# Two-layer-norm matmul on eight cores: coefficient rows copied after the second W block, second pair's results placed elsewhere

## The chip, the cores and the metric

The kernel runs on all 8 cores of one Trainium2 chip. Each core works alone on 1024 of 8192 token rows; nothing is exchanged between cores. The metric is the device time of the slowest core in microseconds (us), as the median of repeated runs. Engine names: TensorE (PE in the profile) multiplies, VectorE (DVE), ScalarE (ACT) and GpSimd (POOL) do the rest, SyncE (SP) only issues transfers. Each engine takes its own instructions strictly in program order, DMA issues and semaphore waits included.

## What is computed

```python
x = L0_attn_x                                  # [1, 8192, 4096], float32
x = x + attn(layernorm(x))                     # one batch entry: softmax over a single element is 1,
                                               # so this is x + layernorm(x) + layernorm(x)
x = x + layernorm(x) @ (aa * tanh(kk * W)).T + bias      # W is [4096, 4096]
```

With one batch entry the attention weighs a single element, so the first step is a per-token scale and shift of x, and the second layer norm is again one. Both are folded into coefficients per token (`cf`, `s1a`, `b1a`). What remains is one matmul of the normalized x with tanh(kk W), plus a residual that is linear in x, plus the bias.

## The kernel before, in words

**Two ways of multiplying.** The first 1024 output columns (`DS`) are made plainly, in two blocks `ot` = 0 and 1 of 512 columns, for 8 token tiles `t`: a closed group (t, ot) is 16 pieces `p` of two matmuls of 512 columns each. The other 3072 columns are made in 12 pairs `j` of 256 columns by a seven-product scheme (`PRODUCTS` M5, M3, M4, M2, M6, M7, M1, 16 matmuls each, 112 a pair), transposed: the product's rows are output columns. This scheme needs sums of quarters of the normalized x (`sA5`, `sA2`, `sA1` and two in place, made once by VectorE, `add_tile`) and sums of blocks of tanh(W) for every pair (`sums`: S6, D12, S1, S7, D21, made by VectorE). Each product is added by VectorE (`take`) into the pair's four result quarters `C(j, q)`, which start as the residual: x transposed, loaded by GpSimd (`load_xt`), times the coefficient row `srow`, plus the row `brow` (`residual`, two GpSimd operations for a quarter). `srow` and `brow` come from TensorE, which spreads the per-token coefficients over all partitions (order entries `("R", 0)` and `("R", 1)`), and from ScalarE, which copies them out of PSUM (`copy_rows(0)`, `copy_rows(1)`).

**Order of TensorE.** `tensor_order` writes it out: token tiles are transposed (`"T"`) as they arrive; block 0 of each follows; in between and after, block 1 of tiles 0 to 4 (`EARLY` = 5) goes piece by piece (`second(p)`), then block 1 of tiles 5 to 7, then the 12 pairs.

**W.** 128 loads of 512 KB (pieces `w`) go through a ring of 4 buffers (`wr`). Pieces 0 to 31 are blocks 0 and 1, then 8 for each pair. SyncE issues the load of piece w when ScalarE has done the tanh of piece w-4. ScalarE does `TANH_BEFORE[t]` pieces before it normalizes its half of tile t, evicts the transposed tile, and goes on; the first rows are copied just ahead of piece 27 and the second just ahead of piece 30. A wait for TensorE's rows therefore holds the tanh, and with it the ring.

**GpSimd's queue.** In program order: half of the normalization, the 8 stores `serve(0..7)` of block 0, the reloads of x for block 1, `load_xt(0, q)` for four quarters, `residual(0, q)`, the 8 stores `serve(8..15)` of block 1 (each waits for VectorE's eviction), `load_xt(1, q)`, `residual(1, q)`, and then for every pair the loads and residuals one and two pairs ahead, where a load waits until ScalarE's store of the pair two before has landed.

**Memory.** Two regions, `early` and `late`, are used again by stage. `base[t]`, the plain results of tile t, stand at `late` 32 + 2t (in units of 512 bf16 columns, two units each). Pair 1's (and every odd pair's) quarters stood at `late` 40 to 47 and its S6 and S7 at 32 and 36. So `load_xt(1, q)` waits for all 8 tiles' results to have landed in memory, and VectorE's S6 of pair 1 waits for those of tiles 0 to 3.

Of the kernel before, what the change touches and what calls it, by code (L numbers as in the profile page):

```python
# [9 lines left out]
F32 = mybir.dt.float32  # L10
# [9 lines left out]
NT = TOK // 128  # L20
# [22 lines left out]

TANH_BEFORE = [1, 4, 7, 10, 13, 16, 20, 23]

# [14 lines left out]
EARLY = 5  # L60

def tensor_order():

    todo = []
# [37 lines left out]
    for p in range(7, PPB):  # L104
        todo += second(p)
        if p in (9, 12):
            todo.append(("R", (9, 12).index(p)))
    for ot in range(1, NO):
# [5 lines left out]
def build_nc():  # L114
# [37 lines left out]

    CT = [[part(early, 32 + 4 * o, 4, F32) for o in range(2)], [part(late, 40 + 4 * o, 4, F32) for o in range(2)]]

# [4 lines left out]
    slot = {}  # L159
    for i, n in enumerate(["B22", "B12", "B11", "B21", "S6", "S7"]):  # L160
        slot[n, 0], slot[n, 1] = part(early, 48 + 4 * i, 4), part(late, 16 + 4 * i, 4)

# [157 lines left out]
    def _(gpsimd):  # L320
# [27 lines left out]
        def load_xt(j, q):  # L348

            if j == 0:  # L350
                gpsimd.wait_ge(s_tr, NCH * NT)
            elif j == 1:
                for t in range(NT):
                    gpsimd.wait_ge(s_y[t], 16 * NO)
            else:
                gpsimd.wait_ge(s_so[j % 2, q], 16 * (j // 2))
            r = 256 * j + 128 * q[1]
            gpsimd.dma_start(C(j, q), xt_h[r:r + 128, 512 * q[0]:512 * (q[0] + 1)]).then_inc(s_xt[j % 2, q], 16)
# [12 lines left out]
        for q in QUARTERS:  # L371
            residual(0, q)
        for i in range(NT, NG):
            serve(i)
        for q in QUARTERS:
            load_xt(1, q)
        for q in QUARTERS:
            residual(1, q)
# [15 lines left out]
    def _(vector):  # L394
# [95 lines left out]
        def sums(j, names):  # L490

            p = j % 2
            for n in names:
# [4 lines left out]
                if n == "S6" and j == 1:  # L498

                    for t in range(4):  # L500
                        vector.wait_ge(s_y[t], 16 * NO)
# [91 lines left out]
    def _(scalar):  # L593
# [43 lines left out]
        while w < W0:  # L637
            if w in (27, 30):
                copy_rows((27, 30).index(w))
            tanh_piece(w)  # L640
            w += 1
        def store(j, q, read):
            scalar.wait_ge(s_rd, READS * j + read)
# [3 lines left out]
        for j in range(NP + 1):  # L647
# [6 lines left out]
            for b in BLOCKS:  # L654
                if j < NP:
                    for k in range(2):
                        scalar.wait_ge(s_w[w % RING], 16 * (w // RING + 1))
                        scalar.activation(slot[b, j % 2][:, k * PW:(k + 1) * PW], wr[w % RING][:, :],  # L658
                                          AF.Tanh, bias=0.0, scale=kk[:, :]).then_inc(s_wt, 1)
                        w += 1  # L660
                if b == "B22" and j >= 2:
                    store(j - 2, (0, 0), 11)
                    store(j - 2, (1, 1), 12)
# [119 lines left out]
```

## Time and profile before

| | |
|---|---|
| runs, median (lowest to highest) | 474.29 us (473.62 to 475.14), 3 runs |
| profiled execution | 478.1 us |
| its span (slowest core, core 3) | 476.6 us |
| spans of the 8 cores | 464.5 to 476.6 us |
| TensorE busy in the span | 433.9 us, 91% |
| VectorE, ScalarE, GpSimd busy | 319.1, 194.2, 203.6 us |

The span is from the first to the last instruction of a core. The profiled execution's own time is 1.5 us above its slowest span and 3.8 us above the median of the runs. A row of a timeline merges neighbours of one kind: start, duration, engine, line, operation, output and inputs by name, how many, and in brackets the idle time ahead of it and what ended that.

### The profile page before, as it was taken

What the parts mean: (1) busy time and instruction counts of PE and PEld (TensorE: products, weight loads), DVE (VectorE), ACT (ScalarE), POOL (GpSimd) and SP (SyncE); (2) the same over time, 40 slices, a digit from 0 to 9 for tenths busy, and PEclk for the clock granted to TensorE, in tenths of its full rate; (3) what the DMA queues carried; (4) which work ended last, traced back from release to release, by engine and by line L of the source; (5) the groups of instructions that cost most, each with busy time, mean ns of one, the idle gap of its engine ahead of it and who ended that gap; (6) DMA issues with size and microseconds to landing.
All of it is one profiled execution on the core that took longest, in us unless ns stands there. A gap on an engine that the chain in (4) does not pass through costs nothing.

```text
span 476.6 us, 7052 instructions; the slowest of 8 cores (464.5 to 476.6 us)
## 1 busy us (share of the span) xinstructions
PE 433.9 (91%) x2184; PEld 205.3 (43%) x2184; DVE 319.1 (67%) x474; ACT 194.2 (41%) x181; POOL 203.6 (43%) x188
## 2 busy tenths in 40 slices
PE   0555899999997999999998999899999999999996
PEld 0533445554543444444443444344444444444442
DVE  2688777687536399998158842978296858584852
ACT  0387777745634604252511541343335242424000
POOL 0132212124153611284366454765566655675620
PEclk9969899999999999999999999999999999999999
DMA  6999999975899878968866976698969796967221
GB/s 134 315 314 302 301 339 290 288 237 157 240 268 289 263 222 242 281 172 343 223 197 227 278 289 221 192 301 287 282 202 305 266 295 218 329 189 270 77 78 45
DMA packets 36612, 116.37 MB, mean 244 GB/s; under 512 B 5088, under 2 KB 5088, under 8 KB 36576
## 3 DMA queue, kind: packets, MB, share of 16 engines
q1 hardware_dynamic: 23472, 84.43, 57.2%
q0 software_dynamic: 5760, 18.88, 13.9%
q10 hardware_dynamic: 7344, 12.62, 7.1%
q8 instruction: 18, 0.29, 0.3%
q14 instruction: 18, 0.15, 0.1%
HBM read 99.14 MB, written 16.78 MB: 243 GB/s over the span
## 4 chain that ended last, share of the span: by engine, by line
PE 48%; DMA 22%; issue 7%; DVE 6%; POOLq 5%; DVEq 5%; POOL 4%; ACT 3%; SPq 1%; ACTq 0%
PE acc L735 34%; PE acc L715 12%; DMA early<-x 6%; DMA wr<-wpieces 6%; DMA early<-xt 5%; POOLq L365 5%; PE acc L686 2%; DMA y<-late 2%; DVEq L464 2%; DMA late<-xt 2%; POOL early L366 2%; POOL late L366 2%; DVEq L517 1%; DVE stats L413 1%; DVE early L509 1%
## 5 line engine op out<-in xcount | busy, mean ns | idle before, releaser
L658 ACT ACTIVATE late<-wr,kk_sb 128x1024 bf16<-128x1024 f32 x48 | 52.9, 1142 | 109.1 <-DVE early L519 39.7
L735 PE MATMUL acc<-h2T,late 128*128 128x512 bf16 x384 | 85.2, 379 | 2.6 <-DVE late L509 2.6
L735 PE MATMUL acc<-h2T,early 128*128 128x512 bf16 x384 | 84.8, 379 | 0.0
L658 ACT ACTIVATE early<-wr,kk_sb 128x1024 bf16<-128x1024 f32 x48 | 53.4, 1143 | 73.3 <-DVE early L522 20.4
L522 DVE SCALAR_TENSOR_TENSOR early<-acc,early 128x512 f32<-128x512 f32 x48 | 33.2, 692 | 56.9 <-POOL early L366 31.0
L715 PE MATMUL acc<-early,h2T 128*128 128x512 bf16 x256 | 60.4, 387 | 4.2 <-ACT early L599 4.2
L715 PE MATMUL acc<-late,h2T 128*128 128x512 bf16 x256 | 58.9, 387 | 3.3 <-ACT late L599 3.3
L735 PEld LDWEIGHTS acc<-h2T,late 128*128 128x128 bf16 x384 | 37.4, 98 | 48.6 <-issue 4.0
L735 PEld LDWEIGHTS acc<-h2T,early 128*128 128x128 bf16 x384 | 37.6, 98 | 45.3
L366 POOL TENSOR_TENSOR early<-early 128x512 f32<-128x512 f32 x24 | 36.0, 1499 | 44.3 <-DMA early<-xt 21.9
L509 DVE TENSOR_TENSOR early<-early 128x2048 bf16<-128x2048 bf16 x30 | 44.8, 1495 | 9.5 <-ACT early L658 7.6
L326 POOL TENSOR_SCALAR early<-early,cf 128x1024 bf16<-128x1024 f32 x12 | 17.4, 1453 | 74.8 <-DVE cf L440 74.8
L509 DVE TENSOR_TENSOR late<-late 128x2048 bf16<-128x2048 bf16 x30 | 47.7, 1590 | 1.7
L522 DVE SCALAR_TENSOR_TENSOR late<-acc,late 128x512 f32<-128x512 f32 x48 | 33.2, 692 | 22.8 <-PE acc L735 12.9
L364 POOL TENSOR_TENSOR early<-early 128x512 f32<-128x512 f32 x24 | 32.9, 1373 | 34.8 <-DMA early<-xt 34.8
L364 POOL TENSOR_TENSOR late<-late,early 128x512 f32<-128x512 f32 x24 | 38.4, 1600 | 17.5 <-DMA late<-xt 17.4
L735 PE MATMUL acc<-early 128*128 128x512 bf16 x192 | 43.4, 379 | 0.0
L735 PE MATMUL acc<-early,late 128*128 128x512 bf16 x192 | 43.4, 379 | 0.0
L366 POOL TENSOR_TENSOR late<-late,early 128x512 f32<-128x512 f32 x24 | 35.2, 1468 | 17.8 <-DMA late<-xt 8.6
L715 PEld LDWEIGHTS acc<-late,h2T 128*128 128x128 bf16 x256 | 25.1, 99 | 33.6 <-issue 6.5
L413 DVE BATCH_NORM_STATS2 stats<-early 128x6 f32<-128x512 f32 x48 | 29.6, 680 | 13.4 <-DMA early<-x 12.7
L715 PEld LDWEIGHTS acc<-early,h2T 128*128 128x128 bf16 x256 | 24.5, 99 | 32.4 <-issue 7.0
(58 smaller groups left out, 425.7 us busy)
## 6 DMA issues: line engine op xcount, KB each, us to landing
wr<-wpieces SPq DMA_DIRECT2D x128, 512.0 KB, 8.0
early<-x SPq DMA_DIRECT2D x24, 512.0 KB, 15.4
early<-xt POOLq DMA_DIRECT2D x24, 256.0 KB, 7.1
yt<-early ACTq DMA_DIRECT2D x24, 256.0 KB, 3.7
late<-xt POOLq DMA_DIRECT2D x24, 256.0 KB, 4.6
yt<-late ACTq DMA_DIRECT2D x24, 256.0 KB, 5.9
h2T<-x SPq DMA_DIRECT2D x8, 512.0 KB, 17.8
y<-late POOLq DMA_DIRECT2D x16, 256.0 KB, 5.2
```

The source lines that it names most:

```text
L326: gpsimd.tensor_scalar(h2b[:, c * CW:(c + 1) * CW], x_of[t][:, c * CW:(c + 1) * CW], cf[t % 2][:, 0:1], cf[t % 2][:, 1:2], ALU.mult, ALU.a ...
L364: gpsimd.tensor_tensor(c, c, srow[:, cols], ALU.mult)
L365: gpsimd.drain()
L366: gpsimd.tensor_tensor(c, c, brow[:, cols], ALU.add).then_inc(s_bs[q], 1)
L413: vector.bn_stats(stats[:, 6 * k:6 * k + 6], x_of[t][:, 512 * k:512 * (k + 1)])
L464: vector.drain()
L509: vector.tensor_tensor(slot[out, p], slot[a, p], slot[b, p], op).then_inc(s_wc, 1)
L522: vector.scalar_tensor_tensor(c, bank, float(sign), c, ALU.mult, ALU.add).then_inc(s_rd, 1)
L658: scalar.activation(slot[b, j % 2][:, k * PW:(k + 1) * PW], wr[w % RING][:, :], AF.Tanh, bias=0.0, scale=kk[:, :]).then_inc(s_wt, 1)
L686: mm = tensor.transpose(ptr[i % 2][:, q * 128:(q + 1) * 128], h2b[:, c * CW + q * 128:c * CW + (q + 1) * 128], ident[:, :])
L715: mm = tensor.matmul(acc[bank_of[t, ot]][:, :], h2T[:, t * D + k * 128:t * D + (k + 1) * 128], wp[ot % 2][:, k * 512:(k + 1) * 512], start ...
L735: mm = tensor.matmul(acc[pbank[j, m]][:, :], slot[b, j % 2][:, k * 128:(k + 1) * 128], a[:, :, k * 128:(k + 1) * 128], start=(k == 0), sto ...
```

## The change

Six edits. (1) ScalarE does three more tanh pieces (23, 24, 25) ahead of its half of tile 7. (2) It copies no rows between pieces any more: the first rows are copied after piece 31, the second after the four tanh pieces of B22 and B12 of pair 0. (3) TensorE's second spreading stands one piece row later, after `second(13)` instead of `second(12)`. (4) The odd pairs' quarters move to `late` 32 to 39, over the results of tiles 0 to 3; S6 and S7 of odd pairs move to 40 and 48. (5) `load_xt(1, q)` waits for tiles 0 to 3 only and is issued after store 12, ahead of the stores 13 to 15. (6) VectorE's S6 of pair 1 waits for tiles 4 and 5 instead of 0 to 3.

```diff
-TANH_BEFORE = [1, 4, 7, 10, 13, 16, 20, 23]
+TANH_BEFORE = [1, 4, 7, 10, 13, 16, 20, 26]
...
-        if p in (9, 12):
-            todo.append(("R", (9, 12).index(p)))
+        if p in (9, 13):
+            todo.append(("R", (9, 13).index(p)))
...
-    CT = [..., [part(late, 40 + 4 * o, 4, F32) for o in range(2)]]
+    CT = [..., [part(late, 32 + 4 * o, 4, F32) for o in range(2)]]
...
-        slot[n, 0], slot[n, 1] = part(early, 48 + 4 * i, 4), part(late, 16 + 4 * i, 4)
+        slot[n, 0], slot[n, 1] = part(early, 48 + 4 * i, 4), part(late, (16, 20, 24, 28, 40, 48)[i], 4)
...
             elif j == 1:
-                for t in range(NT):
+                for t in range(4):
                     gpsimd.wait_ge(s_y[t], 16 * NO)
...
-        for i in range(NT, NG):
+        for i in range(NT, NT + EARLY):
             serve(i)
         for q in QUARTERS:
             load_xt(1, q)
+        for i in range(NT + EARLY, NG):
+            serve(i)
         for q in QUARTERS:
             residual(1, q)
...
                 if n == "S6" and j == 1:
-                    for t in range(4):
+                    for t in range(4, 6):
                         vector.wait_ge(s_y[t], 16 * NO)
...
         while w < W0:
-            if w in (27, 30):
-                copy_rows((27, 30).index(w))
             tanh_piece(w)
             w += 1
+        copy_rows(0)
...
                         w += 1
+                if b == "B12" and j == 0:
+                    copy_rows(1)
```

What the edits do to ScalarE's row of work around tile 7, before. L599 is a tanh piece of the two plain blocks, L607 the normalization, L617 the eviction of the transposed tile, L635 a copy of coefficient rows, L658 a tanh piece of the pairs:

```order
L599 ACTIVATE late<-wr,kk_sb 128x1024 x3
L607 ACTIVATE early<-early,cf 128x1024 x2
L617 COPY h2T<-acc 128x1024 x4
L599 ACTIVATE late<-wr,kk_sb 128x1024 x4
L635 COPY early<-acc 128x512 x2
L599 ACTIVATE late<-wr,kk_sb 128x1024 x3
L635 COPY early<-acc 128x512 x2
L599 ACTIVATE late<-wr,kk_sb 128x1024 x2
L658 ACTIVATE early<-wr,kk_sb 128x1024 x8
```

And of the change, the same place (lines 601, 609, 619, 637 and 659 are the same statements):

```order
L601 ACTIVATE late<-wr,kk_sb 128x1024 x6
L609 ACTIVATE early<-early,cf 128x1024 x2
L619 COPY h2T<-acc 128x1024 x4
L601 ACTIVATE late<-wr,kk_sb 128x1024 x6
L637 COPY early<-acc 128x512 x2
L659 ACTIVATE early<-wr,kk_sb 128x1024 x4
L637 COPY early<-acc 128x512 x2
L659 ACTIVATE early<-wr,kk_sb 128x1024 x4
```

Three tanh pieces moved ahead of the normalization of tile 7, and both pairs of copies moved behind all tanh of block 1.

GpSimd's queue between the residual of pair 0 and that of pair 1, before. L334 is a store of plain results, L358 a load of x transposed, L364 and L366 the two operations of a residual quarter; s_y are the landed stores of a tile:

```order
L366 TENSOR_TENSOR early<-early 128x512
L334 DMA y<-late 128x512 [waits s_ev] x8
L358 DMA late<-xt 128x512 [waits s_y0,s_y1,s_y2,s_y3,s_y4,s_y5,s_y6,s_y7] x4
L364 TENSOR_TENSOR late<-late,early 128x512 [waits s_xt101]
L366 TENSOR_TENSOR late<-late,early 128x512
```

And of the change:

```order
L366 TENSOR_TENSOR early<-early 128x512
L334 DMA y<-late 128x512 [waits s_ev] x5
L358 DMA late<-xt 128x512 [waits s_y0,s_y1,s_y2,s_y3] x4
L334 DMA y<-late 128x512 [waits s_ev] x3
L364 TENSOR_TENSOR late<-late,early 128x512 [waits s_xt101]
L366 TENSOR_TENSOR late<-late,early 128x512
```

The four loads now stand ahead of the last three stores and wait for four tiles instead of eight; the residual operations still stand behind all stores.

TensorE around the two spreadings (L700, later L703), before; L715 (L718) are the plain matmuls:

```order
L715 MATMUL acc<-late,h2T 128x512 x30
L700 MATMUL acc<-early,ones 128x512 x6
L715 MATMUL acc<-late,h2T 128x512 x30
L700 MATMUL acc<-early,ones 128x512 x6
L715 MATMUL acc<-late,h2T 128x512 x126
```

And of the change:

```order
L718 MATMUL acc<-late,h2T 128x512 x30
L703 MATMUL acc<-early,ones 128x512 x6
L718 MATMUL acc<-late,h2T 128x512 x40
L703 MATMUL acc<-early,ones 128x512 x6
L718 MATMUL acc<-late,h2T 128x512 x116
```

The second spreading moved ten matmuls down.

## Rows read from the trace of the kernel before

**Rows 1.** The head of the page.

```profile
span 476.6 us, 7052 instructions; the slowest of 8 cores (464.5 to 476.6 us)
```

**Rows 2.** Span and mean granted TensorE clock of core 6.

```profile
core 6: 472.9 us, clock 0.974
```

**Rows 3.** Timeline of TensorE, core 3: start, duration, what, idle ahead.

```profile
118.62 1.06 PE L686 MATMUL acc<-ident_sb,early 128*128 128x128 bf16 x16
...
152.88 24.73 PE L715 MATMUL acc<-late,h2T 128*128 128x512 bf16 x106 [3.29 <-ACT late L599]
177.45 3.62 PE L735 MATMUL acc<-early 128*128 128x512 bf16 x16
...
205.07 7.07 PE L735 MATMUL acc<-h2T,late 128*128 128x512 bf16 x32
```

**Rows 4.** What TensorE waited for after 130 us, core 3: total us, times, longest.

```profile
PE acc L715 <- ACT late L599: 3.3, 1, 3.3
PE acc L735 <- DVE late L509: 2.6, 3, 1.3
PE acc L735 <- DVE early L509: 1.3, 2, 0.9
```

**Rows 5.** The same view of core 6, its only wait.

```profile
PE acc L715 <- ACT late L599: 2.4, 1, 2.4
```

**Rows 6.** Timeline of ScalarE, core 3.

```profile
108.13 3.23 ACT L599 ACTIVATE late<-wr,kk_sb 128x1024 bf16<-128x1024 f32 x3
114.10 2.37 ACT L607 ACTIVATE early<-early,cf 128x1024 bf16<-128x1024 f32 x2 [2.75 <-DVE cf L440]
...
136.95 1.23 ACT L635 COPY early<-acc 128x512 f32<-128x512 f32 x2 [9.28 <-PE acc L700]
138.08 3.23 ACT L599 ACTIVATE late<-wr,kk_sb 128x1024 bf16<-128x1024 f32 x3
...
151.59 1.15 ACT L599 ACTIVATE late<-wr,kk_sb 128x1024 bf16<-128x1024 f32 x1 [4.59 <-DMA wr<-wpieces]
```

**Rows 7.** Load of W piece 25, core 3: issue time, and time to landing.

```profile
L291 SPq DMA_DIRECT2D wr<-wpieces x1: 328/328/328, 110.4 to 110.4; - x1
...
DMA to landing us min/median/max: 7.3/7.3/7.3
```

**Rows 8.** The same load on core 6.

```profile
L291 SPq DMA_DIRECT2D wr<-wpieces x1: 327/327/327, 112.4 to 112.4; - x1
...
DMA to landing us min/median/max: 4.6/4.6/4.6
```

**Rows 9.** Timeline of TensorE, core 6: transposes of tile 7.

```profile
120.61 1.06 PE L686 MATMUL acc<-ident_sb,early 128*128 128x128 bf16 x16
```

**Rows 10.** Timeline of GpSimd, core 3.

```profile
196.90 0.55 POOL L358 DMA_DIRECT2D late<-xt  x1 [9.70 <-DMA y<-late]
...
201.37 1.27 POOL L364 TENSOR_TENSOR late<-late,early 128x512 f32<-128x512 f32 x1 [1.11 <-DMA late<-xt]
...
214.40 1.26 POOL L366 TENSOR_TENSOR late<-late,early 128x512 f32<-128x512 f32 x1
...
241.74 1.26 POOL L366 TENSOR_TENSOR early<-early 128x512 f32<-128x512 f32 x1 [1.92 <-issue]
```

**Rows 11.** Timeline of VectorE, core 3.

```profile
163.55 2.54 DVE L509 TENSOR_TENSOR early<-early 128x2048 bf16<-128x2048 bf16 x2 [7.61 <-ACT early L658]
...
203.29 3.58 DVE L509 TENSOR_TENSOR late<-late 128x2048 bf16<-128x2048 bf16 x2
...
243.22 1.48 DVE L522 SCALAR_TENSOR_TENSOR early<-acc,early 128x512 f32<-128x512 f32 x2 [15.14 <-PE acc L735]
```

**Rows 12.** Line 509 (the block sums), 180 to 320 us: ns min/median/max.

```profile
L509 DVE TENSOR_TENSOR late<-late x15: 1215/1225/2267, 198.4 to 315.3; 128x2048 bf16<-128x2048 bf16 x15
```

**Rows 13.** Transfers by line, from the page: KB each, median us to landing.

```profile
wr<-wpieces SPq DMA_DIRECT2D x128, 512.0 KB, 8.0
early<-x SPq DMA_DIRECT2D x24, 512.0 KB, 15.4
```

More of the change, by code:

```diff
@@ L151, in build_nc @@
     sA5, sA2, sA1 = part(early, 0, 16), part(early, 16, 16), part(late, 0, 16)
-    CT = [[part(early, 32 + 4 * o, 4, F32) for o in range(2)], [part(late, 40 + 4 * o, 4, F32) for o in range(2)]]
+    CT = [[part(early, 32 + 4 * o, 4, F32) for o in range(2)], [part(late, 32 + 4 * o, 4, F32) for o in range(2)]]
     def C(j, q):
```

## The prediction, as made before the change was run

> **What bounds the kernel now.** I read the page first: the span is 476.6 us, that of core 3 [rows 1]. Then the waits of TensorE on core 3: after 130 us it stands still for three reasons only, 3.3 us for a tanh of ScalarE and 2.6 and 1.3 us for block sums of VectorE (line 509) [rows 4]. That makes 7.2 us; all the rest of that stretch is matmul after matmul, so TensorE is the bound, and a microsecond there counts only if it is one of these 7.2 or a new one. Core 6, with a span of 472.9 us [rows 2], has but one of the waits, 2.4 us for the same tanh [rows 5]. So cores differ, and the time is that of the slowest.
>
> The timelines tell where the two kinds come from. The tanh wait stands at 152.88 us, ahead of the last piece row of block 1 [rows 3]. ScalarE had no data: its last tanh of the block began at 151.59 us after 4.59 us of waiting for the W load [rows 6]. That load goes out when piece 27 is done, and piece 27 began at 138.08 us, because ScalarE had stood 9.28 us for TensorE's coefficient rows before it [rows 6]. The wait for the rows emptied the W ring.
>
> The waits for VectorE start at GpSimd. Its loads for pair 1 went out at 196.90 us, after 9.70 us in which it waited for the last plain stores to land; so the last of those was issued by 187.2 us. Its residual of pair 1 ran from 201.37 to 215.7 us [rows 10]. From there it is late for all that follows: the second residual quarter of pair 2 was finished by the operation at 241.74 us [rows 10], and VectorE, idle for 15.14 us, took pair 2's first product at 243.22 us [rows 11]. The row puts this idle time down to TensorE, but the product had ended near 229 (TensorE starts a product every (205.07 - 177.45) / 8 = 3.45 us, so product M5 of pair 2 runs from 225.8 to 229.2 [rows 3]). What came last was GpSimd. With 14 us lost, VectorE handed over its sums too late five times.
>
> **The change, part by part.** (a) No rows between the tanh pieces. Pieces 26 to 31 follow the eviction of tile 7. Piece 27 is then done some 11 us sooner than now, and so is the load of piece 31, where 3.3 us were missing: all of that wait goes, on core 6 too. The copies themselves (1.23 us for two [rows 6]) are the same work elsewhere. The second spreading waits for the first copies, which come right after the first spreading at 137 us plus, or when piece 31 is done. Piece 31 is asked for when 27 is done, near 128 us; even at the 15.4 us of an x load [rows 13] the copies would be through by 128 + 15.4 + 1.15 + 1.23 = 146 us. TensorE comes to the last piece row at 152.88 - 3.29 = 149.6 us now [rows 3], and the second spreading stands ten matmuls (24.73 / 106 x 10 = 2.3 us) and its own six ahead of it, so at 147.8 us with the 1.8 us of (b). Cost: nothing; with that cover gone, what the copies are late.
>
> (b) Three more tanh pieces ahead of tile 7's normalization. That is the price. Piece 25 is loaded at 110.4 us on core 3 and lands 7.3 us later, at 117.7 [rows 7]; its issue hangs on the tanh of piece 21 (in the group at 108.13 [rows 6]) and doesn't move. Its tanh takes 1.15 us and half of a normalization 2.37 / 2 = 1.2 us [rows 6], so the first quarter of tile 7 is ready at 120.05 us instead of 115.3. TensorE wants it at 118.62 [rows 3]: 1.5 us of new wait with the hand-over. ScalarE then has the second half of the normalization to do before it evicts the first transposes; I add 0.3 us and get 1.8. On core 6 the load of piece 25 goes out at 112.4 us and lands 4.6 us later [rows 8]; 117.0 + 1.15 + 1.2 = 119.4, ahead of the 120.61 us at which its TensorE arrives [rows 9]: nothing there. Bounds of this cost: nothing, and, with the landing of the x loads of the same size, 15.4 us instead of 7.3 [rows 13], 9.9 us. I take the rows' own 1.8 since the load is issued as before; piece 27's load, issued 1.1 us after piece 26's instead of after tile 7, comes behind it.
>
> (c) The second spreading 2.3 us later, and 1.8 us from (b), hold VectorE's second sum of quarters, on which its next work follows. But VectorE then stood 7.61 us before its first block sums at 163.55 us, waiting for a tanh [rows 11], that (a) brings 10 us forward. It starts them at 163.55 - 7.61 + 4.1 = 160.0, 3.5 us sooner. TensorE reaches the pairs 3.3 - 1.8 = 1.5 us sooner, so VectorE gains 2 us on it.
>
> (d) Pair 1's loads ahead of the last three stores. They wait for the stores of tiles 0 to 3 only. With up to 9.7 us for a store to land [rows 10], I put their issue near 176 us and their landing before the last store. The residual of pair 1 then follows that store, near 182 us instead of 201.37: 19 us sooner, done by 182 + 14.3 = 196. Behind them in GpSimd's queue stand the three stores; these wait for evictions later than that anyway. From here every load of pair 2 waits for ScalarE's store of pair 0 instead of GpSimd's backlog. M5 of pair 2 could be taken up to 14 us late before a wait arose; 14.0 us late is what it is now, and I expect under 3. The 3.9 us of waits for line 509 go.
>
> (e) VectorE's sum S6 of pair 1 now waits for the store of tile 5, issued third from last, near 176; it lands by 186. VectorE comes to it behind pair 0's takes, at 198.4 now [rows 12] and 3.5 us sooner then: hidden by 8 us. The new places themselves cost nothing: sizes are as before.
>
> (f) GpSimd's residual of pair 1 now runs beside VectorE's sums from 182 to 196 us. A sum in line 509 takes 1.215 us at least, and up to 2.267 [rows 12]. The two sums at 203.29 us, beside that residual, took 3.58 instead of 2.43 [rows 11]. I give it 2 us in all. These two end at 206.9 now, 206.9 - 3.5 + 2 = 205.4 after, and TensorE wants them for M4 of pair 1, at 205.07 + 3.45 = 208.5 now and 207.0 after [rows 3]. 1.6 us are left. Bounds: nothing, or each of the eight residual operations of 1.27 us [rows 10] held against VectorE in full, 10.2 us.
>
> The Trainium skill, SBUF — State Buffer, section "SBUF: two separate sides", speaks against this part: the port pair that VectorE and GpSimd share is an exclusive lock for a whole instruction, for VectorE operations with two SBUF inputs too. The longest sum of line 509, 1.05 us over the shortest [rows 12], is about what a lock held through a residual operation would do; by that rule in its worst case the sum has the 10.2 us of (f), as the fourth rival below has it.
>
> **The sum.** Core 3: 476.6 - 3.3 - 3.9 + 1.8 = 471.2. Core 6: 472.9 - 2.4 = 470.5. The slowest falls by 5.4 us. The profiled execution is 478.1 us, 3.8 above the median of the runs shown, so its slowest core has perhaps more of these waits than the slowest of a usual run. If that were like core 6, it would gain 2.4. I take 4.3, between the two and nearer to the worked sum: 474.3 - 4.3 = **470.0 us**.
>
> **The rivals.** First, the forecast with a slowest core like core 6: 2.4 us, 471.9 us. For it: the 3.8 us between the profile and the runs. Second, only the tanh wait goes: VectorE, shared with GpSimd, is as late for the sums as now, since TensorE came sooner too. Core 3 then gains 3.3 - 1.8 = 1.5, time 472.8 us. For it speaks the thin 1.6 us of (f). Against it: the five waits now follow a lateness of 14 us. Third, slower: piece 25 lands late, as it shares the transfers with one more load. The place is the transposes of tile 7. At 15.4 us to landing [rows 13], core 3 pays 9.9 us for the 7.2 it gains: 476.6 + 2.7, which is 477.0 us in a run. It decides from 12.7 us to landing on; below that it only shortens the gain. Against it: 7.3 and 4.6 us are what this load took [rows 7, 8], in a stretch with few transfers. Fourth, the 10.2 us of (f): the two sums would end at 213.6, and M4 of pair 1 wait 6.6 us; core 3 stands at 477.8, a run at 475.5 us. Fifth, the change doesn't do what it says: the stores of tiles 0 to 3 land so late that the loads hold the last three stores and the residual starts no sooner. Then it gives the time of the second.
>
> **How the numbers follow.** Forecast 0.58; first rival 0.15; second and fifth together 0.14; third 0.06; fourth 0.07. A measurement of this kernel tells from no change about 0.3%, 1.4 us. Faster by more than that: forecast and first rival, and half of the second, 0.80. Within it: the other half, and some of the fourth, 0.12. Slower: third and the rest of the fourth, 0.08. The forecast's own range is 467.5 to 471.5. Range: from 466.3, all 7.2 us and no new wait with a little beside, up to 473.4, past the second rival.
>
> **What would show it.** In the profile after: no wait for ScalarE in line 718 after 130 us; one of 1 to 2 us at tile 7's transposes on core 3, none on core 6; the tanh pieces of block 1 all done by 136 us; pair 1's residual from about 182 us; VectorE's idle time ahead of pair 2's first take under 8 us, and no wait of TensorE for line 509 after 220 us. Wrong would be: a tile 7 wait over 3 us on several cores, waits for block sums in pairs 0 and 1, or spans that fall on core 3 while another core, from its first 70 us, holds the time.

## The result, and the profile after

The changed kernel takes 478.1 us, the kernel before 474.29 us, medians of 9 runs each: a ratio of 1.0081, interval 1.0045 to 1.0117. It is slower by 0.8%; 470.0 us was forecast, with a chance of 0.80 of a gain.
The profiled execution of the changed kernel took 478.21 us, close to its median; that of before was 3.8 us above its own. So the equal spans of the two profiles don't mean equal times:

```profile
span 476.6 us, 7034 instructions; the slowest of 8 cores (463.5 to 476.6 us)
```

What TensorE waited for after 108 us on the slowest core, now core 2 (total us, times, longest):

```profile
PE acc L738 <- DVE late L511: 5.0, 4, 2.2
PE acc L738 <- DVEq L582: 2.3, 1, 2.3
PE acc L738 <- DVEq L568: 1.4, 1, 1.4
PE acc L689 <- ACT early L609: 0.7, 1, 0.7
PE acc L738 <- DVE early L511: 0.2, 1, 0.2
```

Against [rows 4] the wait for a tanh (there line 599, here it would be line 601) is gone. In its place stand 8.9 us of waits for VectorE instead of 3.9. L511 is the line of the block sums (509 before); L582 is where VectorE reports sA1, the sum of tiles that the last product of pair 0 reads; L568 is its report of the tile differences ahead of it. Together 9.6 us, where core 3 of before had 7.2.

Where they fall, from TensorE's timeline on core 2:

```profile
116.77 1.05 PE L689 MATMUL acc<-ident_sb,early 128*128 128x128 bf16 x16 [0.74 <-ACT early L609]
...
185.87 7.07 PE L738 MATMUL acc<-h2T,early 128*128 128x512 bf16 x32 [1.37 <-DVEq L568]
195.26 5.29 PE L738 MATMUL acc<-late,early 128*128 128x512 bf16 x16 [2.33 <-DVEq L582]
...
210.69 3.61 PE L738 MATMUL acc<-h2T,late 128*128 128x512 bf16 x16 [2.24 <-DVE late L511]
```

Tile 7 costs 0.74 us, below the 1.8 us of the forecast. The rest begins where the pairs begin, and falls in pairs 0 and 1. That is VectorE's and GpSimd's stretch, so I read their timelines next. VectorE, core 2:

```profile
161.89 7.84 DVE L490 TENSOR_TENSOR h2T<-h2T 128x2048 bf16<-128x2048 bf16 x4
169.91 4.24 DVE L511 TENSOR_TENSOR early<-early 128x2048 bf16<-128x2048 bf16 x2 [0.19 <-issue]
...
185.90 1.48 DVE L524 SCALAR_TENSOR_TENSOR early<-acc,early 128x512 f32<-128x512 f32 x2 [0.45 <-issue]
...
202.04 2.54 DVE L511 TENSOR_TENSOR late<-late 128x2048 bf16<-128x2048 bf16 x2 [5.39 <-DMA y<-late]
```

The first row is the first four of the eight in-place differences of the transposed input, the second two block sums behind them (S7 and D21). The same two groups before, on core 3 (lines 488 and 509):

```profile
170.68 4.62 DVE L488 TENSOR_TENSOR h2T<-h2T 128x2048 bf16<-128x2048 bf16 x4
175.49 2.54 DVE L509 TENSOR_TENSOR early<-early 128x2048 bf16<-128x2048 bf16 x2 [0.19 <-issue]
```

The four differences took 4.62 us then and 7.84 us now, the two sums 2.54 and 4.24. VectorE had begun the pairs' work well ahead: its first block sums (S6 and D12) start at 153.77 us on core 2, against 163.55 [rows 11]. From there to the first take, at 185.90 against 187.68 us, it has no idle time worth naming in either kernel, and 8.0 of the 9.8 us are lost: 3.2 and 1.7 in the two groups above, 1.1 in the fifth difference and 1.0 in each of two plain results. GpSimd, core 2, tells why:

```profile
155.92 1.50 POOL L364 TENSOR_TENSOR early<-early 128x512 f32<-128x512 f32 x1 [15.48 <-DMA early<-xt]
162.79 1.44 POOL L366 TENSOR_TENSOR early<-early 128x512 f32<-128x512 f32 x1 [5.37 <-issue]
...
175.42 2.07 POOL L366 TENSOR_TENSOR early<-early 128x512 f32<-128x512 f32 x1
177.44 2.72 POOL L334 DMA_DIRECT2D y<-late  x5
189.49 0.55 POOL L358 DMA_DIRECT2D late<-xt  x1 [9.33 <-DMA y<-late]
...
192.12 1.61 POOL L334 DMA_DIRECT2D y<-late  x3
194.97 1.26 POOL L364 TENSOR_TENSOR late<-late,early 128x512 f32<-128x512 f32 x1 [1.24 <-DMA late<-xt]
204.46 1.27 POOL L366 TENSOR_TENSOR late<-late,early 128x512 f32<-128x512 f32 x1 [8.23 <-issue]
```

Pair 0's residual (lines 364 and 366, eight operations) runs from 155.92 to 177.5 us, on top of VectorE's differences and sums from 161.89 on. Before, on core 3, it ran from 147.31 to 161.4, its last four operations in the 7.61 us in which VectorE stood idle for a tanh [rows 11]; the block sums and differences from 163.55 on ran without it. The stores 8 to 12 (block 1 of tiles 0 to 4) go out in one heap at 177.44, since they stand behind this residual. Those of before, on core 3:

```profile
147.31 1.55 POOL L364 TENSOR_TENSOR early<-early 128x512 f32<-128x512 f32 x1 [7.66 <-DMA early<-xt]
152.00 1.27 POOL L366 TENSOR_TENSOR early<-early 128x512 f32<-128x512 f32 x1 [3.13 <-issue]
...
161.38 1.12 POOL L334 DMA_DIRECT2D y<-late  x2
```

The first two left at 161.38 us then, the others as VectorE had their results. So pair 1's loads now leave at 189.49 us and the store of tile 5, which VectorE's S6 of pair 1 now waits for, behind them; VectorE stands 5.39 us for it at 202.04.

Why did the residual of pair 0 start so late? Its four loads were issued at about the same time, 138.3 to 139.9 us against 137.5 to 139.1; counted from tile 7's transposes that is 2.6 us later, and the larger part is the landing. Their landing after (core 2), and then before (core 3):

```profile
DMA to landing us min/median/max: 17.5/18.9/21.9
```

```profile
DMA to landing us min/median/max: 9.7/10.7/11.9
```

I read it so that the W loads, which ScalarE now lets go earlier, share the transfers with them. One experiment below (x4) bears on it; it was not measured apart, and stays argued.

To compare kernels without the differences of single cores, I took from each profile the mean over its 8 cores, counted from the start of tile 7's transposes (T). "Pairs" is TensorE's first product, "sums" VectorE's first block sums, "take" its first take, R0 and R1 the residuals of pairs 0 and 1, "waits" the sum of TensorE's waits after 108 us. The kernels e1 to x4 are those of the experiments below.

```
kernel   pairs  sums   take   R0 start, length   R1 start   waits
before   56.2   42.2   66.8   27.9, 14.8         78.1       3.5
after    53.8   37.3   67.2   35.8, 19.5         73.2       4.1
e1       53.7   37.4   66.6   34.9, 19.3         78.1       3.9
e2       54.9   41.8   66.4   27.8, 14.8         66.0       2.8
e3       53.7   37.6   66.6   34.2, 18.8         68.9       3.4
e4       53.8   38.1   66.8   29.8, 23.8         70.1       3.9
e5b      53.8   37.4   65.1   34.4, 14.9         65.1       4.7
e6b      55.3   42.0   66.4   27.9, 14.1         76.7       2.0
e7b      53.8   37.0   61.1   35.6,  9.1         61.4       0.9
e8b      55.4   43.1   67.2   27.8,  6.4         76.6       2.5
e9       53.7   41.5   70.1   37.2, 18.6         73.9       6.1
x1       53.7   37.5   75.8   34.5, 15.3         65.9       3.8
x2       56.0   42.3   72.7   28.0, 14.0         75.8       2.1
x4       53.7   41.1   72.1   29.1, 13.3         74.4       1.7
```

TensorE reaches the pairs 2.4 us sooner after the change, and VectorE starts its block sums 4.9 us sooner; its first take is no sooner. That difference is the case. (In x1, x2 and x4 the first take was moved behind other work, so theirs is another thing.)

A wait of TensorE can cost more than its length. On core 2 the 16 matmuls behind the wait of 2.33 us took 5.29 us, others 3.61. The granted clock, the last figure but two of this row of busy times, was 0.57 of full speed there, so mostly the lower of the two levels, and 1.00 in the 4 us before and after:

```profile
195.00:199.00 4.00, 3.74 (x10) 1.40 (x11) 1.39 (x2) 0.00 (x0) 1.22 (x1) 0.57 1.06 242
```

Five of the eight cores have one such group in the pairs, 1.4 to 1.7 us longer. Before, on core 3, the same stood behind the 3.29 us for the tanh [rows 3]: 0.58 from 153 to 157 us. In e7b, where no core waits over 1.1 us in the pairs, seven cores end 348.0 to 348.2 us after T; after the change they end 349.3 to 359.8 us after it.

### The profile page after: what moved, and what is told of

The parts are those of the page before. It is cut to its first block, busy times and chain, and to the rows that moved or that the text cites. A ratio compares the mean times of both kernels' runs of the same rounds, so it can differ in the third digit from the quotient of the medians.

```text
span 476.6 us, 7034 instructions; the slowest of 8 cores (463.5 to 476.6 us)
## 1 busy us (share of the span) xinstructions
PE 435.8 (91%) x2184; PEld 205.6 (43%) x2184; DVE 328.0 (69%) x474; ACT 193.7 (41%) x181; POOL 207.7 (44%) x188
## 3 DMA queue, kind: packets, MB, share of 16 engines
q0 software_dynamic: 5760, 18.88, 14.9%
## 4 chain that ended last, share of the span: by engine, by line
PE 44%; DMA 25%; issue 10%; POOLq 7%; POOL 6%; DVE 3%; DVEq 2%; SPq 2%; ACT 1%; ACTq 0%
PE acc L738 34%; DMA early<-xt 8%; PE acc L718 8%; DMA wr<-wpieces 8%; POOLq L365 6%; DMA y<-late 4%; DMA early<-x 3%; POOL early L366 3%; DMA late<-xt 2%; POOL late L366 2%; PE acc L689 2%; SPq L285 2%; DVEq L519 1%; DVEq L507 1%; ACT early L609 1%
## 5 line engine op out<-in xcount | busy, mean ns | idle before, releaser
L718 PE MATMUL acc<-early,h2T 128*128 128x512 bf16 x256 | 61.7, 393 | 2.9 <-ACT early L601 2.9
L738 PEld LDWEIGHTS acc<-h2T,late 128*128 128x128 bf16 x384 | 37.3, 98 | 51.3 <-issue 7.1
L718 PE MATMUL acc<-late,h2T 128*128 128x512 bf16 x256 | 57.0, 379 | 0.0
L366 POOL TENSOR_TENSOR early<-early 128x512 f32<-128x512 f32 x24 | 36.5, 1522 | 46.3 <-DMA early<-xt 22.6
L364 POOL TENSOR_TENSOR early<-early 128x512 f32<-128x512 f32 x24 | 37.1, 1548 | 41.5 <-DMA early<-xt 41.4
L511 DVE TENSOR_TENSOR late<-late 128x2048 bf16<-128x2048 bf16 x30 | 48.0, 1600 | 7.0 <-DMA y<-late 5.4
L511 DVE TENSOR_TENSOR early<-early 128x2048 bf16<-128x2048 bf16 x30 | 48.4, 1615 | 1.8 <-issue 0.2
L524 DVE SCALAR_TENSOR_TENSOR late<-acc,late 128x512 f32<-128x512 f32 x48 | 33.2, 692 | 21.9 <-POOL late L366 11.5
L366 POOL TENSOR_TENSOR late<-late,early 128x512 f32<-128x512 f32 x24 | 35.5, 1479 | 24.5 <-issue 12.2
L364 POOL TENSOR_TENSOR late<-late,early 128x512 f32<-128x512 f32 x24 | 37.3, 1555 | 17.1 <-DMA late<-xt 17.0
L718 PEld LDWEIGHTS acc<-early,h2T 128*128 128x128 bf16 x256 | 24.8, 100 | 32.4 <-issue 7.4
L718 PEld LDWEIGHTS acc<-late,h2T 128*128 128x128 bf16 x256 | 24.8, 98 | 28.8
```

Of the source, the lines that this page charges most:

```text
L364: gpsimd.tensor_tensor(c, c, srow[:, cols], ALU.mult)
L366: gpsimd.tensor_tensor(c, c, brow[:, cols], ALU.add).then_inc(s_bs[q], 1)
L511: vector.tensor_tensor(slot[out, p], slot[a, p], slot[b, p], op).then_inc(s_wc, 1)
L524: vector.scalar_tensor_tensor(c, bank, float(sign), c, ALU.mult, ALU.add).then_inc(s_rd, 1)
L718: mm = tensor.matmul(acc[bank_of[t, ot]][:, :], h2T[:, t * D + k * 128:t * D + (k + 1) * 128], wp[ot % 2][:, k * 512:(k + 1) * 512], start ...
L738: mm = tensor.matmul(acc[pbank[j, m]][:, :], slot[b, j % 2][:, k * 128:(k + 1) * 128], a[:, :, k * 128:(k + 1) * 128], start=(k == 0), sto ...
```

## The experiments

**One half at a time.** e1 is the kernel before with ScalarE's edits alone, e2 with the edits to memory places, GpSimd's order and the waits alone.

```diff
 # e1, on the kernel before
-TANH_BEFORE = [1, 4, 7, 10, 13, 16, 20, 23]
+TANH_BEFORE = [1, 4, 7, 10, 13, 16, 20, 26]
...
-        if p in (9, 12):
+        if p in (9, 13):
...
-            if w in (27, 30):
-                copy_rows((27, 30).index(w))
...
+        copy_rows(0)
...
+                if b == "B12" and j == 0:
+                    copy_rows(1)
 # e2: the changed kernel with these lines as before
```

> The kernel before with the edits to ScalarE and to the second spreading alone. Theory A (the W loads, let go earlier, crowd the loads of pair 0's x transposed, so GpSimd's residual of pair 0 starts late and runs beside VectorE's sums; both come late to pairs 0 and 1): most of the loss is here. The residual of pair 0 starts 5 us or more later against tile 7's transposes than before (about 35 instead of 28 us after them), lasts about 20 instead of 15 us, and the time is 2 to 4 us above before. Theory B (the loss comes from GpSimd's new order: pair 1's loads hold the last three stores, and S6 of pair 1 waits for tile 5's store): this kernel has none of it and gains the tanh wait of 2 to 3 us: 471.5 to 473 us.

> The kernel before with the edits to memory, GpSimd's order and the waits for stores alone. Theory A: the residual of pair 0 is as early as before, the loads of pair 1 go out 15 us sooner, no wait of VectorE for a store, TensorE's waits after 200 us go: 470.5 to 473.5 us. Theory B: VectorE waits for the store of tile 5 here too, time 2 to 4 us above before.

Measured on one chip, before at 473.76 us: e1 476.24 us, ratio 1.0047 (1.0016 to 1.0078); e2 474.25 us, ratio 0.9999 (0.9973 to 1.0026). ScalarE's edits alone make the kernel slower, as the first theory had it; GpSimd's alone change nothing in the time, which neither theory had expected. e1 on its slowest core (1) shows the stretched differences and the same kind of waits, with no move of stores or loads in it:

```profile
164.28 8.02 DVE L488 TENSOR_TENSOR h2T<-h2T 128x2048 bf16<-128x2048 bf16 x4
```

```profile
PE acc L736 <- DVE early L509: 2.3, 1, 2.3
PE acc L736 <- DVE late L509: 2.3, 1, 2.3
PE acc L736 <- DVEq L580: 1.8, 1, 1.8
PE acc L687 <- ACT early L607: 1.4, 1, 1.4
```

In e2 the GpSimd edits do what they say: on core 0 the loads of pair 1 go out at 172.80 us, and the residual starts right behind the last store.

```profile
172.80 0.55 POOL L358 DMA_DIRECT2D late<-xt  x1 [3.70 <-DMA y<-late]
...
184.45 1.28 POOL L364 TENSOR_TENSOR late<-late,early 128x512 f32<-128x512 f32 x1
```

Its residual of pair 1 starts 12 us sooner by the table, and the time is the same. The waits tell why. Those for block sums fell, in the mean of the cores from 1.5 to 0.5 us; those for sA1 rose from 0.2 to 1.2 us. The earlier residual runs beside the four additions of sA1, which took 4.62 us before. On core 1, VectorE and TensorE:

```profile
184.94 7.83 DVE L490 TENSOR_TENSOR late<-h2T 128x2048 bf16<-128x2048 bf16 x4
```

```profile
PE acc L737 <- DVEq L582: 4.1, 1, 4.1
```

So what (d) of the forecast gained was paid again at another sum of VectorE.

**The wait for tile 5's store.** e3 exchanges the places of S6 and S7 of the odd pairs, so that S6 lands where no store is awaited and S7, taken up later, waits for tiles 4 and 5.

```diff
-        ..., part(late, (16, 20, 24, 28, 40, 48)[i], 4)
+        ..., part(late, (16, 20, 24, 28, 48, 40)[i], 4)
...
-                if n == "S6" and j == 1:
+                if n == "S7" and j == 1:
```

> The changed kernel with the places of S6 and S7 of odd pairs exchanged, so that the later S7 waits for tiles 4 and 5 and S6 for nothing. Theory A: VectorE's wait of up to 5.8 us at S6 goes, but its lateness in pair 0 stays: 1 to 2 us under the changed kernel, 476 to 477 us. Theory B: the whole loss goes, 472 to 474 us.

Measured beside e1: 476.62 us, 1.0047 (1.0013 to 1.0082). VectorE's wait falls to this, on core 1:

```profile
DVE late L511 <- DMA y<-late: 0.4, 1, 0.4
```

The ratio is that of e1. So of the changed kernel's 0.8%, 0.5% is ScalarE's part and the remaining 0.3% fits the S6 wait; with intervals of 0.3% each that overlap, and the changed kernel timed at another time, this split is not shown, only likely.

**Pair 0's loads first.** e4 issues pair 0's residual loads ahead of the reloads of the base tiles, so that pair 0's residual can start sooner.

```diff
+        for q in QUARTERS:
+            load_xt(0, q)
         for i in range(NT):
             load_res(closed[i][0])
...
-        for q in QUARTERS:
-            load_xt(0, q)
```

> The changed kernel with the four loads of pair 0's x transposed issued ahead of the eight reloads of x for block 1. Theory A: they land 5 to 10 us sooner, the residual of pair 0 starts near 150 us again once the rows are there and all behind it follows: 470 to 474 us. Theory B: stores 13 to 15 are still held by pair 1's loads: less than 1 us under the changed kernel, 477 us or more.

Measured beside e1: 476.56 us, 1.0052 (1.0022 to 1.0082), which neither theory had. The residual started 6 us sooner than after the change, at T + 29.8, and then lasted 23.8 us instead of 19.5. On core 4:

```profile
147.97 1.57 POOL L366 TENSOR_TENSOR early<-early 128x512 f32<-128x512 f32 x1 [8.17 <-ACT early L637]
157.67 2.27 POOL L368 TENSOR_TENSOR early<-early 128x512 f32<-128x512 f32 x1 [8.13 <-issue]
```

GpSimd did the first operation and then stood for 8.13 us in its drain, before the second. Nothing in the profile is named for it; the times of the transfers point to them, in the last section. The next pair of runs follows from it.

**The drain.** e5 is the changed kernel and e6 the kernel before, with the drain between multiply and add replaced by a semaphore of GpSimd's own.

```diff
-            gpsimd.tensor_tensor(c, c, srow[:, cols], ALU.mult)
-            gpsimd.drain()
+            gpsimd.tensor_tensor(c, c, srow[:, cols], ALU.mult).then_inc(s_gp, 1)
+            done[0] += 1
+            gpsimd.wait_ge(s_gp, done[0])
```

**Pair 0's residual made short.** e7 is the changed kernel and e8 the kernel before, each with the operations of pair 0's residual on 8 of each 512 columns; the other 504 keep the plain load and are left out of the computation. Loads, waits and the number of operations stay. e8 is the control.

```diff
+            if j == 0:
+                c, cols = C(j, q)[:, 0:8], slice(512 * q[0], 512 * q[0] + 8)
```

> The changed kernel with GpSimd's drain between the two residual operations replaced by a semaphore that the first raises and GpSimd itself waits for. Theory C (the drain ends only when every transfer that GpSimd has issued has landed; in four traces the operation behind it starts 0.5 to 1.0 us after the last landing; in the changed kernel the three stores ahead of pair 1's residual hold it): the idle time of 8 us inside the first residual quarter of pair 1 goes, that residual ends 8 us sooner, the same in pair 0 (5 us) and 2 to 4 us in the pairs after; time 1 to 3 us under the changed kernel's 478.1. Theory B' (the idle time is VectorE's hold on the shared port, not the transfers): it stays, time the same.

> The kernel before with the same replacement. Theory C: the idle time of 3.1 us in pair 0 and 1.9 us in pairs 1 and 2 behind the first operation goes; GpSimd gains on VectorE and TensorE's waits for line 509 after 240 us shrink: 472 to 473.5 us against 474. Theory B': no difference.

> The changed kernel with the residual operations of pair 0 on 8 of 512 columns, so that nearly all of their GpSimd time is left out (pair 0's output lacks it). Theory A (VectorE is as late in pair 0 as before, though its tanh comes sooner, because GpSimd's residual of pair 0 now runs beside VectorE's sums and each holds the other up): VectorE's sums of line 490 take 1.2 us each instead of 2, pair 0's first take comes 4 us sooner against tile 7's transposes (63 instead of 67 us after), TensorE's wait at the last product of pair 0 goes, and the stores 8 to 12 go out about 15 us sooner; time 471 to 474 us. Rival D (VectorE is late because the second spreading stands later, not by contention): the take stays 66 to 67 us after the transposes, time above 475.5.

> The kernel before with the same work left out, as the control. Theory A: there the residual of pair 0 ran while VectorE stood 7.6 us for a tanh, so little is gained: within 1 us of before. Rival D: the same gain here as in the changed kernel.

There is no ratio for this first set. The slowest of cores 4 to 7, mean and standard error, was 472.42 +- 0.55 us before, 473.83 +- 0.35 for e5 (one of its eight runs, at 495.1, left out), 469.71 +- 0.46 for e6, 466.84 +- 0.26 for e7 and 473.74 +- 0.86 for e8. The same kernels were run again on another chip (before: 476.04 us there), e6 on a third (474.71 us):

> The changed kernel with the semaphore in place of the drain, for its time over all eight cores. If the drain's wait for the stores is a part of the loss, 1 to 2 us under the changed kernel: 476 to 477 us. If the waits only gather at pair 0's last product, as the undisturbed die showed (waits of 4 us there), it is no more than 1 us under it: 477 to 478 us.

> The changed kernel with pair 0's residual operations on 8 of 512 columns (the rest of them left out), over all eight cores. Theory A, as the undisturbed die showed it (slowest of its cores 466.8 us against 472.4 of before): 468 to 470 us, so that the overlap of GpSimd's residual with VectorE's sums is worth the whole loss and more.

> The kernel before with the same left out, the control, over all eight cores: no gain, 473 to 476 us.

> The kernel before with the semaphore in place of the drain, once more. On the undisturbed die it was 2.7 us under before (469.7 to 472.4 us for its slowest core). Expected now: 471.5 to 473 us against 474.

Measured: e5b 476.87 us, 1.0021 (0.9995 to 1.0048). e6b 472.18 us, 0.9945 (0.9919 to 0.9971). e7b 470.56 us, 0.9897 (0.9859 to 0.9935). e8b 476.60 us, 1.002 (0.9984 to 1.0056).

e7b against e8b is the finding. Without pair 0's residual the changed kernel is 1.0% faster than the kernel before, where with it it was 0.8% slower; the kernel before gains nothing by the same edit. On core 7 of e7b, VectorE and then TensorE:

```profile
162.61 4.64 DVE L492 TENSOR_TENSOR h2T<-h2T 128x2048 bf16<-128x2048 bf16 x4
167.44 2.54 DVE L513 TENSOR_TENSOR early<-early 128x2048 bf16<-128x2048 bf16 x2 [0.19 <-issue]
```

```profile
PE acc L740 <- DVE late L513: 1.1, 1, 1.1
```

The differences take 4.64 us again and the sums 2.54; the first take comes at T + 61.1, 6 us sooner, and TensorE's waits fall to 0.9 us in the mean. This is what the forecast had promised for ScalarE's edits, but it had left GpSimd's residual out of it. e7b also lets the stores behind the residual go sooner (R1 at 61.4), so the 1.8% between it and the changed kernel is the price of both together; how it divides is not shown, and e3, where only the wait for a store is gone, suggests that the stores are the smaller part.

The Trainium skill, SBUF — State Buffer, section "SBUF: two separate sides", says that VectorE and GpSimd share a port pair under an exclusive lock. The trace agrees, with 4.64 us alone and 7.84 beside the residual for the same four operations; GpSimd's own operations went from 1.27 us [rows 10] to 2.07. For a lock, and against a sharing by amount, speaks e7b, where an operation of GpSimd on 8 columns took 0.20 us between VectorE's sums (at 168.68 us, core 7) and up to 1.27 us beside its differences and sums, about as long as one of them (1.22 us):

```profile
162.67 1.22 POOL L368 TENSOR_TENSOR early<-early 128x8 f32<-128x8 f32 x1 [4.57 <-issue]
```

In e5b the idle time between multiply and add is gone, on core 4:

```profile
157.26 1.26 POOL L366 TENSOR_TENSOR early<-early 128x512 f32<-128x512 f32 x1 [15.02 <-DMA early<-xt]
158.66 2.06 POOL L369 TENSOR_TENSOR early<-early 128x512 f32<-128x512 f32 x1
```

and the residuals are short (14.9 us). Still it gains only to 1.0021, and what remains stands in two rows of the same core:

```profile
PE acc L741 <- DVEq L585: 5.4, 1, 5.4
PE acc L692 <- ACT early L612: 1.8, 1, 1.8
```

L585 is the report of sA1. Pair 1's residual now came sooner, onto the additions of sA1, as in e2:

```profile
191.32 8.68 DVE L493 TENSOR_TENSOR late<-h2T 128x2048 bf16<-128x2048 bf16 x4
```

In the kernel before the same edit is a gain of 0.55%. So the chain of VectorE up to sA1 is what TensorE meets once it comes sooner.

**The early tanh taken back.** e9 is the changed kernel with the last entry of TANH_BEFORE at 23, as before, which takes away the wait at tile 7 and moves pieces 23 to 25 behind it.

> The changed kernel with 23 tanh pieces ahead of tile 7 as before, instead of 26. TensorE's wait at tile 7's transposes (0 to 1.2 us in the changed kernel, 1.7 at most in the run with the edits to ScalarE alone) goes on every core; piece 31 still comes in time. Where this wait adds to the time: 0.5 to 1 us under the changed kernel, 477 to 477.6. Where the third load fewer ahead gives pair 0's loads of x room: more, down to 476.

Measured: 478.78 us, 1.0061 (1.0028 to 1.0094), on the chip of e5b. The gain that was expected is not there. On core 1:

```profile
PE acc L738 <- DVE late L511: 4.0, 1, 4.0
PE acc L738 <- DVEq L582: 3.4, 1, 3.4
```

The wait at tile 7 is gone, but the run isn't a clean test of it. With the three pieces back behind tile 7 the tanh of pair 0 comes later too: VectorE stands 3.6 us for it on core 1 before its first block sums, which start at T + 41.5 instead of 37.3, its first take at T + 70.1 instead of 67.2, and TensorE waits 6.1 us in the mean instead of 4.1. By the waits the three pieces ahead are worth their small price; the times of e9 and the changed kernel, taken apart from each other, don't tell.

**A version made from this.** If the chain to sA1 is what is late, it can be made shorter. x1 (on the changed kernel) and x2 (on the kernel before) have the semaphore of e5 and do the sums S1 and sA1 of pair 0 ahead of the takes that stood before them (and no longer behind). x4 is x2 with the coefficient rows copied ahead of tanh pieces 28 and 31 instead of 27 and 30: a small step of what the change does in full.

```diff
+            if j == 0:
+                vector.wait_ge(s_mm, nth_product[0, "M5"])
+                sums(0, ["S1"])
+                vector.wait_ge(s_grp, NG)
+                for i in range(4):
+                    add_tile(i, tiles(sA1), quarter(0, 0), quarter(1, 1), ALU.add)
+                vector.drain().then_inc(s_sa, 1)
             vector.wait_ge(s_bs[0, 1], j + 1)
...
 # x4 alone
-            if w in (27, 30):
-                copy_rows((27, 30).index(w))
+            if w in (28, 31):
+                copy_rows((28, 31).index(w))
```

> The changed kernel with the semaphore in place of the drain, and VectorE making pair 0's S1 and the third sum of quarters (sA1) ahead of its takes of M5 and M3. Theory A says that with the drain gone the wait of 4 us stands at pair 0's last product alone, for that sum; 3 us of it go: TensorE's waits after tile 7 under 2 us in all, 470 to 473 us against 474 of before. If it stays, the sum is not what TensorE waits for there: 475 us or more.

> The kernel before with both: the semaphore for the drain, and the early sum. What is left is the tanh wait of 0.4 to 4.4 us: 471 to 473 us.

> As the one before, with the rows copied ahead of pieces 28 and 31 instead of 27 and 30, so that the load of piece 31 is not held by the rows, while the tanh pieces of pair 0 stay as late as before and GpSimd's residual still runs while VectorE waits for them. Theory A: the tanh wait goes and VectorE's is not called up by it, since its sum is early: 470 to 472 us, under the one before by 1 to 2. If lateness of VectorE simply takes the place of the tanh wait: the same as the one before.

Measured on one chip with e6b (before 474.71 us): x1 472.97 us, 0.997 (0.9947 to 0.9992); x2 472.82 us, 0.9956 (0.9925 to 0.9988); x4 470.57 us, 0.9911 (0.9878 to 0.9944). x1 is under the kernel before, where e5b, on another chip, was not. x2 is no better than e6b, 0.9945: as long as TensorE itself waits for the tanh, on core 1

```profile
PE acc L720 <- ACT late L604: 3.7, 1, 3.7
```

the shorter chain of VectorE has nothing to give. In x4 both waits, for the tanh and for sA1, are off the path; core 5, its slowest, has this one wait after 108 us:

```profile
PE acc L740 <- DVE late L512: 1.1, 1, 1.1
```

and ScalarE there waits for the rows one piece later than before, with the next load already in:

```profile
137.00 1.23 ACT L640 COPY early<-acc 128x512 f32<-128x512 f32 x2 [6.19 <-PE acc L705]
...
145.90 1.15 ACT L604 ACTIVATE late<-wr,kk_sb 128x1024 bf16<-128x1024 f32 x1
```

Its residual of pair 0 starts at T + 29.1, near the 27.9 of before, not at 35.8: with W's loads spread much as before, pair 0's loads land 7.8 to 12.0 us after issue on core 5. x4 is 0.9% faster than the kernel before; its runs lie from 469.5 to 471.1 us, those of e6b from 470.3 to 473.0, and those of x2 reach 475.2. No run has the semaphore and the moved rows without the early sums, so what the early sums add in x4 is not shown.

## Why the prediction was wrong

**(a) No rows between the tanh pieces.** Right. No core waits for ScalarE in line 718 any more, and TensorE reaches the pairs 2.4 us sooner. The wait on core 3 was even worth more than the 3.3 us of the sum, since the granted clock was 0.58 behind it.

**(b) Three more pieces ahead of tile 7, 1.8 us.** The mechanism was right and the size fair: 0.74 us on core 2, 1.4 on core 1 of e1, 1.8 on core 4 of e5b. The other cores of the changed kernel have 0.3 us, 1.2 us or nothing. Whether taking it away alone would give time, e9 doesn't tell, since it moves VectorE's tanh as well.

**(c) "VectorE's first block sums 3.5 us sooner".** This is the step that failed. The sums did start sooner, by 4.9 us in the mean, but the forecast took it that all behind them moves with them. I put the work in VectorE's idle time of 7.61 us and kept every duration as it was. In that idle time half of GpSimd's residual of pair 0 had run alone. The residual came later (loads at 17.5 to 21.9 us to landing instead of 9.7 to 11.9) and VectorE sooner, so they met; VectorE's work up to the first take grew by 8.0 us on core 2, and the first take did not move against T. In the sum, 3.9 us of waits for VectorE were to go; on the slowest core there are 8.9 instead. I had weighed this very cost in (f) for pair 1, and for pair 0 it stood at nothing. e1 shows the loss with ScalarE's edits alone, e7b and e8b that it hangs on this residual.

**(d) Pair 1's loads ahead of the last three stores.** Half right. They go ahead, but at 189.49 us and not 176, so the residual starts at 194.97 against 201.37 [rows 10], 6.4 us sooner where I had 19, and loses 8.23 us in a drain right behind. "These wait for evictions later than that anyway" was true before; with pair 0's residual ending at 177.5 it is GpSimd that holds the stores. Where it worked, in e2, the 12 us took a mean 1.0 us of waits for block sums away and added as much at sA1.

**(e) S6 behind tile 5's store, "hidden by 8 us".** Failed by the same lateness: 5.39 us of VectorE's time. e3 takes it away, for perhaps 0.3%.

**(f) Pair 1's residual beside VectorE's sums, 2 us.** Right in kind. In the changed kernel the residual was so late that it hardly came to bear there; in e2 and e5b, where it was early, it did, with up to 4.1 and 5.4 us of TensorE's time, and at sA1, which (f) had not looked at.

The rivals: the third (tile 7 late) named a place where it did not happen. The fourth had the right mechanism, the lock between VectorE and GpSimd, but in pair 1; in the changed kernel it struck in pair 0. The fifth came half true: the loads held the last three stores (192.12 us), yet the residual started sooner. The second, that VectorE is as late as before because TensorE comes sooner too, describes the traces best, but it priced this as a gain of 1.5 us.

Open stays how e1's 0.5% divides. TensorE's waits in the means are 3.9 us, against 2.0 to 2.8 in kernels whose ScalarE is as before (e2, e6b, e8b). Over all its runs the mean core's span is 1.4 us longer than that of the kernel before on the same chip (469.5 against 468.1 us), which the 1 to 2 us of waits cover; the rest of the 2.5 us between the medians lies in the slowest core being further above the mean. Its slowest core in the profile also has one group of matmuls that took 1.7 us longer behind a wait. One profile a kernel does not tell more, and the profile of before, at 3.5, was of an execution above its median.

## What to carry to other kernels

When an edit removes a wait, look at what other engines did while the waiting engine stood still: two engines that share a resource may have been kept apart by just that idle time, and durations read from the old trace no longer hold. Before bringing the bounding engine forward, find what it will meet next and shorten that first: the change lost 0.8%; a semaphore in place of the drain, a shorter VectorE chain and a small step of the change gained 0.9% together, of which the semaphore alone had 0.55%.

## What the runs showed of the hardware that was not expected

```profile
L334 POOL DMA_DIRECT2D y<-late x3: 539/544/544, 192.1 to 193.2; - x3
...
DMA to landing us min/median/max: 9.8/10.6/10.7
```

```profile
L490 DVE TENSOR_TENSOR h2T<-h2T x8: 1215/1748/2291, 161.9 to 184.2; 128x2048 bf16<-128x2048 bf16 x8
```
